# A graph convolution on one core: more gathered rows on two side queues

## What is computed

```
h   = relu(layernorm(x))                                  # x: 12500 x 128
W   = (ssp(edge_attr @ w1 + b1) @ w2 + b2) * C(edge_weight)   # 212500 edges, 50 -> 128
msg = (h @ lin1)[src] * W                                 # gather 212500 rows of 512 B
agg = segment_sum(msg, dst)                               # dst is sorted
out = x + ssp(agg @ lin2 + b) @ lin + b'                  # ssp(x) = softplus(x) - ln 2
```

## Time and profile before

| | |
|---|---|
| median of 3 runs | 2022.07 us (2021.86 to 2024.72) |
| profiled execution | 2022.45 us, of which the span in the trace is 2020.7 us |
| POOL busy | 1517.5 us (75%) |
| PE busy | 1341.8 us (66%), mean granted clock 0.82 |
| DVE busy | 1048.1 us (52%) |
| ACT busy | 792.7 us (39%), row issues not counted |

### The profile page before, as it was taken

The page is one execution under the profiler, slowest core; times in us unless marked ns, Lnnn a source line. Parts: engine busy times, 40 slices in busy tenths (PEclk is TensorE's granted clock), DMA queues, the critical chain, the costliest instruction groups (busy, mean ns, idle before and its releaser), DMA issues.

```text
span 2020.7 us, 48993 instructions
## 1 busy us (share of the span) xinstructions
PE 1341.8 (66%) x12880; PEld 1108.7 (55%) x12881; DVE 1048.1 (52%) x3153; ACT 792.7 (39%) x925; POOL 1517.5 (75%) x1611
## 2 busy tenths in 40 slices
PE   5577667776776777676666666666666666666666
PEld 5465556655555556555555555555555555555454
DVE  8664655555545555555544444444544444445454
ACT  5764333333434443433343333333333334333332
POOL 7777777777777777777777777777777777777775
PEclk9887888888888878888787888778877878887887
DMA  9633343333343344334333233333333333333322
GB/s 320 247 94 92 89 97 88 98 98 92 92 99 97 88 97 99 87 93 102 87 88 97 77 97 90 84 98 81 92 94 80 98 86 88 97 88 87 96 76 51
DMA packets 114579, 202.33 MB, mean 100 GB/s; under 512 B 36409, under 2 KB 69917, under 8 KB 114173
## 3 DMA queue, kind: packets, MB, share of 16 engines
q0 software_dynamic: 51392, 105.35, 21.6%
q1 hardware_dynamic: 55228, 91.86, 14.7%
q10 hardware_dynamic: 7680, 1.98, 0.7%
HBM read 186.25 MB, written 12.80 MB: 99 GB/s over the span
## 4 chain that ended last, share of the span: by engine, by line
POOL 38%; ACTq 19%; issue 18%; ACT 16%; PE 4%; DVE 3%; DMA 1%; DVEq 0%; SPq 0%; POOLq 0%
POOL XG L460 38%; ACTq L576 17%; ACT TB L593 5%; ACT TB L587 4%; ACT TB L590 4%; ACTq L565 1%; PE PW L878 1%; ACT XG L482 1%; DMA XG<-xp_scratch,IX 1%; PE PA L897 1%; DVE XG L776 1%; DVE TB L651 1%; DVE SCR L630 1%; PE PX L824 1%; PE PX L862 0%
## 5 line engine op out<-in xcount | busy, mean ns | idle before, releaser
L460 POOL DMA_INDIRECT XG<-xp_scratch,IX x1542 | 1455.6, 944 | 470.6 <-issue 463.0
L776 DVE SCALAR_TENSOR_TENSOR XG<-PW,CC,XG 128x128 f32<-128x128 f32 x1602 | 453.1, 344 | 435.3 <-DMA XG<-xp_scratch,IX 399.6
L587 ACT ACTIVATE TB<-PX 128x1024 f32<-128x1024 f32 x208 | 212.8, 1023 | 1039.8 <-PE PX L862 532.9
L875 PE MATMUL PW<-BPB,ones 128*128 128x512 bf16 x415 | 183.7, 443 | 563.3 <-DVE XG L776 558.8
L878 PEld LDWEIGHTS PW<-W,TB 128*128 128x128 f32 x3314 | 545.9, 234 | 20.0
L878 PE MATMUL PW<-W,TB 128*128 128x128 f32 x3314 | 548.9, 320 | 0.0
L731 DVE SCALAR_TENSOR_TENSOR TB<-PX,TB 128x1024 f32<-128x1024 f32 x208 | 254.2, 1222 | 347.1 <-ACT TB L593 336.5
L875 PEld LDWEIGHTS PW<-BPB,ones 128*128 128x128 bf16 x415 | 41.2, 99 | 674.2 <-issue 670.2
L897 PE MATMUL PA<-OH,XG 128*64 128x64 f32 x6408 | 296.1, 259 | 0.0
L897 PEld LDWEIGHTS PA<-OH,XG 128*64 128x64 f32 x6408 | 265.4, 171 | 31.3 <-issue 18.4
L862 PE MATMUL PX<-AT,W 51*128 51x256 f32 x1662 | 258.2, 432 | 2.6 <-ACT XG L482 2.6
(11 more groups left out here) (107 smaller groups left out, 538.1 us busy)
## 6 DMA issues: line engine op xcount, KB each, us to landing
HA<-xp_scratch ACTq DMA_DIRECT2D x3840, 0.5 KB
AT<-attr_b SPq DMA_DIRECT2D x104, 512.0 KB
HT<-xp_scratch SPq DMA_DIRECT2D x3092, 0.5 KB
XG<-xp_scratch,IX POOLq DMA_INDIRECT x1542, 2.7
AG<-zero SPq DMA_DIRECT2D x1, 6400.0 KB, 21.6
xp_scratch<-XG SPq DMA_DIRECT2D x24, 256.0 KB
XR<-x SPq DMA_DIRECT2D x24, 256.0 KB
out<-XR SPq DMA_DIRECT2D x24, 256.0 KB, 3.8
```

The lines of the kernel that those rows point to most:

```text
L460: e.indirect_dma_start(XG[q % XG_N][0:p, k * D:(k + 1) * D], None, xp, bass.IndirectOffsetOnAxis(ap=IX[0:p, t0 + k:t0 + k + 1], axis=0)).t ...
L587: e.activation(T, PXP[pair % 2][:, :], ACT.Abs).then_inc(s_ab, 1)
L776: ins = e.scalar_tensor_tensor(out=G, in0=weights(q)[0:p, k * D:(k + 1) * D], scalar=CC[0:p, t0 + k:t0 + k + 1], in1=G, op0=ALU.mult, op1= ...
L875: e.matmul(P[0:p, 0:n * D], ones[:, 0:p], BP[0][:, 0:n * D], start=True, stop=False, skip_group_check=True)
```

## The change

SP fetches 44 rows a turn instead of 32, with two register loads of 22 addresses instead of four of 8. A tile can now begin in the middle of a load, so the address table `SI` is laid out by turns (101 rows of 44) and no longer by tiles. ACT fetches 22 rows a pair instead of 20: four behind Abs, four behind Exp (three and three before), 14 behind Ln as before. The sets of quads follow from the two numbers. SP's tiles: 34 instead of 25 (4244 rows), one every 11.6 quads instead of every 16. ACT's tiles: 33 instead of 30 (4224 rows). POOL's gathers of L460: 1530 instead of 1542.

```diff
-ROWS = 32
-NH = (NCH - 3 - 2) * ROWS // TILE
-HQ = {18 + (j + 1) * TILE * CHQ // ROWS: j for j in range(NH) if 18 + (j + 1) * TILE * CHQ // ROWS < NQ - 2}
+ROWS = 44
+TURNS = NCH - 3
+HQ = {18 + -(-(j + 1) * TILE // ROWS) * CHQ: j for j in range((TURNS - 2) * ROWS // TILE)}
+HQ = {q: j for q, j in HQ.items() if q < NQ - 2}
...
-PAIR_ROWS = 20
+PAIR_ROWS = 22
...
-        SI = sb("SI", [NH, TILE], i32)
+        SI = sb("SI", [TURNS, ROWS], i32)
...
-            def fetch(a, b):
-                n = a
-                while n < b:
-                    j, p = n // TILE, n % TILE
-                    m = min(8 - n % 8, b - n)
-                    if p == 0 and j >= HT_N:
-                        e.wait_ge(s_sc, HAND[j - HT_N] + 1)
+            def fetch(turn):
+
+                for h in range(0, ROWS, ROWS // 2):
+                    n0 = turn * ROWS + h
+                    if n0 >= END:
+                        return
                     _, at = nc.values_load_multi_w_load_instructions(
-                        SI[j:j + 1, p:p + m], engines=[mybir.EngineType.SP], min_val=0, max_val=ROW * (NODES - 1),
+                        SI[turn:turn + 1, h:h + ROWS // 2], engines=[mybir.EngineType.SP], min_val=0, max_val=ROW * (NODES - 1),
...
-                    for i, v in enumerate(at):
-                        e.dma_start(HT[j % HT_N][p + i:p + i + 1, :].bitcast(u8), row(v)).then_inc(s_r[j % HT_N], 16)
-                    n += m
+                    for n, v in zip(range(n0, END), at):
+                        j, p = n // TILE, n % TILE
+                        if p == 0 and j >= HT_N:
+                            e.wait_ge(s_sc, HAND[j - HT_N] + 1)
+                        e.dma_start(HT[j % HT_N][p:p + 1, :].bitcast(u8), row(v)).then_inc(s_r[j % HT_N], 16)
...
                     e.activation(T, PXP[pair % 2][:, :], ACT.Abs).then_inc(s_ab, 1)
-                    fetch(3)
+                    fetch(4)
                     e.wait_ge(s_ab, pair + 1)
                     e.activation(T, T, ACT.Exp, scale=-1.0).then_inc(s_ex, 1)
-                    fetch(3)
+                    fetch(4)
...
                     numbers((i - FIRST) // 2)
-                    fetch(PAIR_ROWS - 6)
+                    fetch(PAIR_ROWS - 8)
...
-        "src_h": _np.ascontiguousarray(tiles(g["src"]).T[[quad(q)[0] for q in HAND]]),
+        "src_h": turns(tiles(g["src"]).T[[quad(q)[0] for q in HAND]], TURNS, ROWS),
```

More of the change, by code:

```diff
@@ L423, in _ @@
                 load(k)
-                fetch(min(END, (k - AT_N) * ROWS), min(END, (k - AT_N + 1) * ROWS))
+                fetch(k - AT_N)
                 while c < NNC and (k - AT_N) * CHQ >= starts(c) + 6:
```

## The result

The changed kernel takes 2362.06 us (median of 4 runs, 2361.29 to 2362.54), the kernel before 2023.39 in the same series: ratio 1.1669, 95% interval 1.1649 to 1.1689. It is 17% slower. The forecast was 2007.1, the range ended at 2021.

What follows compares the result with a forecast made beforehand. POOL, full with gathers of L460, was taken to set the end. 12 fewer gathers at 1.249 us take 15.0 us off 2022.45, giving 2007.5, or 2007.1 after 0.4 for the median; range 2004.5 to 2021.

Steps and rivals of the forecast that it cites:

- POOL's part: POOL's gathers of L460: 12 fewer at an unchanged 1.249 us each, 15.0 us off the end.
- the price of a register load of 22: SP's and ACT's address loads: 0.056 us a value, so 1.576 us on SP and +0.11 us a pair on ACT.
- My bounds for the turn: SP's turn of 44 rows: 16.8 us if more values cost nothing, 20.0 if all scales with rows; sum 18.34.
- The rule of the Trainium skill that I set aside: Register loads on SP and ACT: 200 ns a register even in bulk, from HBM; set against 73 ns each in the trace.
- the two queues' row issues cost their own time alone: Row issues on SP and ACT, each priced by its own queue: pitch 0.321 us on SP, 0.304 on ACT.
- Rival D: SP's queue becomes the bound: 18.9 us a turn with a load at 1.8 us, end at 2035.7 us; chance 16%.
- Exp started 1.24 us after Abs: ACT's pair: with four rows behind Abs, Exp starts 1.30 us after it instead of 1.06, +0.24 us.
- Ln 1.26 after Exp: ACT's pair: with four rows behind Exp, the next pass starts after 1.29 us instead of 1.09, +0.20 us.
- Four rows: ACT's rows behind Abs: begin 0.08 us after it and end at 1.20 us, pitch 0.304 us.
- Without rows the pairs: Last pairs, from 196 on, without rows on ACT: PE sets the pace at 6.45 us a pair.
- The new waits: SP's first row of a tile waits for the scatter three tiles before, up to 8 us if on time; cost nothing.

Runs made afterwards that it cites:

- run 6: Kernel before with SP at 40 rows a turn in two aligned loads of 20, ACT kept at 20 rows: 2015.03 us, ratio 0.9959.
- Experiments 1: Kernel before with only its register loads varied (ACT's start bytes, SP's lengths), same rows fetched: ratio 1.007 on a disturbed chip.
- 2: Changed kernel with loads of 22 kept, second half of each table row moved from byte 88 to 96: 2135.42 us, ratio 1.0556.
- 4: Kernel before with one part of the change each: ACT's part alone 2343.15 us, ratio 1.1591; SP's part alone 2340.13 us, ratio 1.1565.
- 3: Changed kernel with second halves at byte 96 and loads of 24 values, two unused: 2127.48 us, ratio 1.0498.

## Why the prediction was wrong

**POOL's part: right, and beside the point.** 1530 gathers at an unchanged pitch. In run 6, where POOL is still the bound, a gather less is worth what was said.

**The step that failed: the price of a register load of 22.** I drew a line through 8 values (0.79 us) and 20 (1.46) and read 1.58 off it. Both ends were whole groups of four on multiples of 16 bytes, at 0.22 a group by the fit above. 22 is five groups and two singles, 1.9 us, and the second half of each row starts at byte 88, where the time fits every value being fetched singly: 4.9. The mean is 3.4 on SP and 3.6 on ACT, not 1.6. On ACT that is 2.1 us a pair more than the loads of 20, with 0.35 for the later passes: 8.54 + 2.45 = 11.0, measured 11.1. On SP it is 3.7 us a turn: 18.3 + 3.7 = 22.0, measured 22.2 to 22.3. Experiments 1, 2 and 4 show it. My bounds for the turn, 16.8 and 20.0, came from length alone and didn't ask what the change does to the address. Of the 355 us between forecast and result, 227 went when only the start moved (2) and 8 more with loads of 24 (3); 120 stay.

**The rule of the Trainium skill that I set aside** (Runtime: NRT & Kernel Launch, Instruction fetch mechanics, 200 ns a register even in bulk) is stated for loads from HBM. For loads from SBUF that don't start on 16 bytes the runs here come to nearly the same number, 0.21 us a value. My row (73 ns a value) showed the other case alone and couldn't refute it, and I gave the rule no chance. With 0.2 us a value for every load the turn would have come out at 18.34 - 3.15 + 44 x 0.2 = 24.0, an estimate by that page; 22.2 was measured, as only half of the loads pay it.

**A second step failed behind the first, for the 120 us that stay: that the two queues' row issues cost their own time alone.** 8468 rows over the 1760 us in which they were to go are 4.8 a microsecond. Four runs with 40 to 44 rows a pair give 4.35 to 4.5 with a backlog; the kernel before asks for 36 / 8.54 = 4.2 in its first stretch, the changed one for 4.0. With 4.45, 8468 rows take 1903 us from 130 on, and with 100 us of tail behind them 2133: 2127 and 2135 are measured. So by this estimate the forecast of 2007 was out of reach for this split of rows even with free register loads; no run tests that. That the two queues hold each other up is shown (6, and the drawn-out issues in 3). That it is single rows that count, and not all that SP and ACT issue, is a reading of the rates, and what the limit is stays open. The Trainium skill (DMA: Bandwidth & Descriptors, Why a DMA increments its semaphore by 16 and not by 1) says that a transfer issued by SP or ACT runs on the lowest-numbered k of the core's 16 engines, and that each of the k writes the semaphore once. A row has two packets here (8448 in q10 for ACT's 4224 rows), which fits k = 1, the row and one such write. Then all rows of both queues would go through one engine, which would fit a cap at a mean DMA share of 37%; but the trace doesn't name engines, and no run here tests it.

**Rival D had half of the mechanism, and undersized.** SP's queue alone does become the bound, but at 22.2 us a turn and 2340 us (4), not at 18.9 and 2036. But ACT's queue, whose load I made 0.11 us longer, was just as full, and in the changed kernel it is the one that ends last. (A load of 22 at 1.8 us gives 18.8 us a turn by my sum, not 18.9; nothing hangs on it.)

**Smaller terms.** Exp started 1.24 us after Abs (forecast 1.30), Ln 1.26 after Exp (1.29). Four rows took 1.12 us, as summed. Without rows the pairs went at 5.9 us (6.45, from PE's busy time at a mean granted clock of 0.82; it was 0.94 here). The new waits of SP's first rows for a scatter cost nothing: SP was never early enough to meet them.

## What to carry to other kernels

When a register load changes its length, ask what becomes of the start address of the next one: a table cut into pieces should have them padded to whole groups of 16 bytes, and loading two values too many took 0.2 us less than loading two left over. Two durations at tidy sizes don't price an untidy size between or just beyond them. And work moved from a full queue to free ones has a second limit where those queues meet again: add up the rate of both before trusting the time of each. Of the kernels tried, the one that kept to loads of 20 and 40 rows a pair was the only one that gained, 8 us.

## What the runs showed that was not expected

- A load of 20 registers from SBUF takes 1.46 us at bytes 0, 16 and 32, and 4.63 at bytes 4 and 8. 22 values take 1.90 from a multiple of 16 bytes and 4.9 from byte 88, 24 take 1.70 (SP).
- Single 512-byte rows by SP and ACT together went at 4.35 to 4.5 a microsecond at most in the four runs with a backlog, while the mean DMA share was 0.36 to 0.39; the output blocks behind them landed after 12 to 18 us instead of 3.8, and the issues of both queues took longer at times.
- With 44 rows a pair and a padded table the trace gives the gathers a median landing of 10 to 12 us, with 40 and 42 rows one of 2.8 to 2.9, at nearly the same row rate. DVE's list of waits has none for gathers with 44 rows or 42, and 93.1 us with 40. Why they differ stays open.
- The same kernel took 2022 to 2028 us on some chips and 2827 to 2865 on others. On the latter, between a twentieth and a fifth of SP's and ACT's register moves and row issues, whose medians stay at 29 and 213 to 228 ns, take over 0.5 us, mostly 0.7. Why isn't known.
